# A pixel-transformer kernel on one core: among stages of several streams that are ready, the oldest stream's goes next instead of the one ready longest

## The reference

```python
# block 0
x = x + g_msa * attn(rope(q), rope(k), v, mask) @ attn_out_W      # self attention, 1024 x 1024
x = x + g_x * attn(qc, kc, vc) @ co_W                             # cross attention on 77 context rows
x = x + g_mlp * (gelu(xm @ mlp_W1 + b1) @ mlp_W2 + b2)
# block 1
x = x + sigmoid(gate) * (sum_e(router_e * silu(combined @ w1_e) @ w2_e) @ out_w + out_b)
# block 2, the same as block 0 with biases, full self attention over all 1024 keys, no rope
# block 3
x = x_q + attn(adaLN(x_q) @ Wq, k, v) @ Wp                        # cross attention again
```

## Time and profile before

| | us |
|---|---|
| median of 3 runs | 3506.51 (3498.44 to 3508.25) |
| the profiled execution, its own time | 3509.56 |
| its span, first to last instruction | 3507.8 |
| PE busy | 3309.1 |
| DVE busy | 1840.0 |
| ACT busy | 1434.7 |
| mean granted TensorE clock | 0.957 |

### The profile page before, as it was taken

How to read it: one execution, slowest core, us unless ns; L and a number is a source line. 1 busy time by engine, 2 the same in 40 slices (tenths; PEclk the granted TensorE clock), 3 DMA queues, 4 the chain that set the end, 5 groups by cost and what they waited for, 6 DMA issues and landing times.

```text
span 3507.8 us, 49090 instructions
## 1 busy us (share of the span) xinstructions
PE 3309.1 (94%) x19540; PEld 1824.3 (52%) x19540; DVE 1840.0 (52%) x3843; ACT 1434.7 (41%) x2607; POOL 244.4 (7%) x214
## 2 busy tenths in 40 slices
PE   6899999999889999998999999999999999999887
PEld 3555766657575666666333444544455344543364
DVE  4776554552412232324766765467755676556423
ACT  0344434353312222211355455554554645555433
POOL 1100100100100000001000010010100001010010
PEclk9999999989889999999899999999999999999897
DMA  5200000002000000001000000000000000000000
GB/s 166 90 6 1 9 20 4 25 1 95 16 22 1 0 1 0 1 1 55 1 1 1 1 7 4 1 25 7 7 4 16 10 7 7 4 16 16 1 1 13
DMA packets 57257, 57.99 MB, mean 17 GB/s; under 512 B 17728, under 2 KB 51249, under 8 KB 56765
## 3 DMA queue, kind: packets, MB, share of 16 engines
q1 hardware_dynamic: 57028, 54.79, 5.0%
HBM read 46.89 MB, written 7.89 MB: 16 GB/s over the span
## 4 chain that ended last, share of the span: by engine, by line
PE 90%; DVE 7%; ACT 2%; issue 1%; POOL 0%; DMA 0%; DVEq 0%; SPq 0%; ACTq 0%
PE ps L901 82%; PE ps L1075 3%; PE ps L1202 1%; PE ps L1055 1%; PE ps L1066 1%; DVE max_halves L1564 1%; DVE row_max_cross L1717 1%; ACT probs L1943 1%; DVE bn_stats L1618 1%; PE ps L1180 0%; ACT big L1895 0%; DVE big L1723 0%; DVE bn_stats L1595 0%; DVE xn_tok L1631 0%; DVE mean_var L1624 0%
## 5 line engine op out<-in xcount | busy, mean ns | idle before, releaser
L1895 ACT ACTIVATE big<-ps 128x512 f32<-128x512 f32 x1280 | 687.5, 597 | 809.4 <-PE ps L901 808.3
L901 PE MATMUL ps<-big 32*128 32x512 f32 (+2 forms) x5760 | 947.2, 605 | 14.7 <-DVE row_max L1561 4.3
L1564 DVE TENSOR_REDUCE max_halves<-ps 128x1 f32<-128x512 f32 x1024 | 652.8, 684 | 367.5 <-PE ps L901 366.7
L901 PEld LDWEIGHTS ps<-big 32*128 32x128 f32 (+1 forms) x5760 | 390.0, 189 | 496.2 <-issue 388.6
L901 PE MATMUL ps<-big,probs 128*32 128x512 f32 (+1 forms) x2688 | 379.0, 606 | 9.8 <-ACT big L1895 4.1
L901 PE MATMUL ps<-weights_mlp,big 128*128 128x256 f32 (+1 forms) x1248 | 336.0, 422 | 2.5 <-ACT big L1955 2.5
L901 PEld LDWEIGHTS ps<-weights_mlp,big 128*128 128x128 f32 x1248 | 236.9, 192 | 85.1 <-issue 57.1
L1601 DVE TENSOR_TENSOR x_tok<-ps,x_tok 128x512 f32<-128x512 f32 x112 | 77.3, 691 | 304.6 <-PE ps L901 304.6
L901 PE MATMUL ps<-x_T,weights_mlp 128*128 128x256 f32 x1024 | 229.8, 384 | 4.1 <-ACT x_T L1912 4.1
L1943 ACT ACTIVATE probs<-ps 77x512 f32<-77x512 f32 x384 | 196.1, 591 | 88.9 <-PE ps L901 88.9
L1561 DVE TENSOR_REDUCE row_max<-ps 128x2 f32<-128x512 f32 x256 | 165.0, 685 | 126.7 <-PE ps L901 126.3
(11 more groups left out here) (223 smaller groups left out, 3401.0 us busy)
## 6 DMA issues: line engine op xcount, KB each, us to landing
weights_mlp<-in_L_xcond_mlp_W SPq DMA_DIRECT2D x5, 1024.0 KB, 5.3
weights_mlp<-in_L_xcond_W_mlp SPq DMA_DIRECT2D x5, 1024.0 KB, 5.3
x_tok<-in_x SPq DMA_DIRECT2D x4, 1024.0 KB, 9.4
out_y<-x_tok SPq DMA_DIRECT2D x8, 512.0 KB, 2.9
big<-in_L_xcond_e_w SPq DMA_DIRECT2D x3, 1024.0 KB, 10.2
gates_biases<-mod_rows SPq DMA_DIRECT2D x20, 128.0 KB, 5.1
big<-in_L_xcond_adaLN_W SPq DMA_DIRECT2D x1, 2304.0 KB
kc_groups<-x_tok SPq DMA_DIRECT2D x3, 616.0 KB, 8.3
```

Source lines behind the costliest of these rows:

```text
L901: return pe.matmul(out, lhsT, rhs, start=first, stop=last)
L1564: dve.tensor_reduce(NMP[:, e, j, qt, hf:hf + 1], PS[:, bank, :], AX.X, ALU.max, negate=True).then_inc(R.frees(key), 1)
L1895: act.activation(PB[:, score % 2, j, :], PS[:, R.bank(key), :], ACT.Exp, scale=SCALE).then_inc(R.frees(key), 1)
```

## The change

Three lines of `overlapped` change, and one is added.

- The third key of the choice is the number of the stream instead of the time since which the stage has been ready. So of all `o_tokens` streams with a stage that can start, the oldest one's is placed.
- `cs` is now held back as well while a product of another half waits in `OTC` for its transposition. `state["holder"]` remembers whose product that is. A half may still place its own next `cs` between its `cp` and its `ct`.

```diff
-            state = {"now": 0.0, "t": -R.lead, "probs": 0, "turn": 0, "exp": 0.0, "credit": 0.0}
+            state = {"now": 0.0, "t": -R.lead, "probs": 0, "turn": 0, "exp": 0.0, "credit": 0.0, "holder": None}
...
                 if kind == "cs":
-                    return state["probs"] == 0
+                    return state["probs"] == 0 and (state["turn"] == 0 or state["holder"] == (tok[1], tok[2], tok[4]))
...
                     state["turn"] += {"cs": 0, "cp": 1, "ct": -1}[kind]
+                    state["holder"] = (tok[1], tok[2], tok[4]) if kind == "cp" else state["holder"]
...
-                work = sorted([f for f in found if f[0] <= now and cost(R, f[2])], key=lambda f: (not hidden_follows(f[2]), f[1] >= NB, f[0]))
+                work = sorted([f for f in found if f[0] <= now and cost(R, f[2])], key=lambda f: (not hidden_follows(f[2]), f[1] >= NB, f[1]))
```

## The result

The changed kernel takes 3495.86 us, the median of 18 runs (3484.44 to 3511.53). The kernel before takes 3509.19 us in 18 runs beside it (3498.44 to 3521.9). The ratio is **0.9971, 95% interval 0.996 to 0.9981**: about 10 us, or 0.29%, faster. (The two medians differ by 13 us, the means by 11. Runs of one kernel scatter by over 20 us, so the ratio with its interval is what counts.) The forecast was 3510.5 us, a gain of nothing. The time lies in the range that was given (3494 to 3526), but it was reached by a way that no part of the prediction described. Idle time went up as forecast, and the kernel got faster all the same.

The account below looks back on a forecast made before the run. PE was taken to bound the kernel, its work unchanged. Idle terms -2.6 + 2.0 - 2.4 + 1.0 + 4.1 = +2.1 us, x 1.93 = +4.1, on the median 3506.51 gave 3510.5 us; range 3494 to 3526.

Parts of the forecast that it names:

- Layer norm at the end of L0: L0's end piece: PE waits for normalized rows total 7.8 us in place of 3.45, +4.4 us.
- The other kinds there: L0's end piece: waits of `cs` -2.0, `cp` +1.7, `cm` -2.0, short ones -0.1 us; with layer norm +2.0.
- Middle of L2: `cm` directly behind a slot at 22 places in place of 11, usually waiting 0.76 us for exponentials: +4.1 us.
- Last slots of L0: Waits of 1.84 and 0.73 us both go, since `oP` and `oT` of older streams stand between the slots: -2.6 us.
- the rest of that middle: Middle of L0: twice a `cs` has only about 1.7 us between it and `cn`, +1.0 us for both.
- End of L2: L2's end piece: layer norm -2.7, `oT` -1.7, `cs` -1.3, `cp` +6.9, `cm` -2.7, short ones -0.9; together -2.4 us.
- The factor 1.93: Whole kernel: each us of idle time also brings 0.93 us of lost clock, so idle change is multiplied by 1.93.
- 32 products of `m1`: Example of the clock following idle time: they take 9.42 us right behind idle times, 7.14 us elsewhere.
- Tight places: Rival, slower: `ct` behind `cp` and one `cs` in the middles waits at every second place, 3529 us; chance 0.25.
- Table loads: Rival, slower: six more table loads on ACT, all ahead of something PE waits for, 3525 us; chance 0.05.
- Faster, end pieces shorter: Rival: waits on DVE in the end pieces vanish as bare counts say, 3487 us, half of it 3496; chance 0.20.

Follow-up runs that it names:

- the guard alone: The kernel before with only the new hold-back of `cs`, in both regions, and the old key of choice: 3510.68 us, ratio 1.0001.
- new middles alone: New key and hold-back of `cs` only until the last slot of a region, the old rule from there on, against the kernel before: 3512.45 us, ratio 1.0015.
- L0 alone: New key and hold-back of `cs` in L0, the old rule in L2, against the kernel before: 3503.45 us, ratio 0.9986.
- New ends alone: New key and hold-back of `cs` only behind the last slot of each region, against the kernel before: 3493.49 us, ratio 0.9947.
- L2's end alone: New key and hold-back of `cs` only behind the last slot of L2, against the kernel before: 3491.03 us, ratio 0.996.
- L0's end alone: New key and hold-back of `cs` only behind the last slot of L0, against the kernel before: 3512.64 us, ratio 1.0005.

## Why the prediction was wrong

**The idle time: right in its sign and in most of its terms.** The four pieces were to bring +2.1 us and brought +6.5, three times as much, though only 4.4 us more. The terms one by one:
- *Layer norm at the end of L0.* Forecast was one wait of 4.6 us, and `m1` behind it over 8 us. In the changed kernel, PE in order of time:

```profile
982.44 1.94 PE L1076 MATMUL ps<-ident,xn_tok 128*128 128x128 f32 x8 [4.49 <-DVE xn_tok L1632]
985.34 9.06 PE L902 MATMUL ps<-x_T,weights_mlp 128*128 128x256 f32 x32 [0.95 <-ACT x_T L1913]
```

  DVE and POOL just ahead of it. The normalization starts as soon as POOL is done:

```profile
980.82 1.03 POOL L2093 TENSOR_TENSOR rstd<-eps_tile,minus_half 128x4 f32<-128x4 f32 x1
981.88 1.38 DVE L1632 TENSOR_SCALAR xn_tok<-x_tok,mean_var,rstd 128x256 f32<-128x256 f32 x4 [1.47 <-POOL rstd L2093]
```

  All waits for `lnT` of that piece rose from 3.5 to 8.2 us, +4.7 (forecast +4.4). The other kinds there: `cs` -2.3 (-2.0), `cp` +1.8 (+1.7), `cm` -1.4 (-2.0).
- *Middle of L2.* +4.4 (forecast +4.1). The waits of `cm` are 33.2 us in place of 29.8, and those for a slot's exponentials in them 14.6 in place of 9.7:

```profile
L902 PE MATMUL ps<-k_v_cross,x_T 32*128 32x154 f32 x772 | 41.5, 329 | 33.2 <-ACT big L1896 14.6 <-DVE row_max_cross L1718 12.7 <-DVE max_halves L1565 5.8
```

- *Last slots of L0.* -2.6 was said. The 1.84 us is gone, but one of 0.72 us of the other kind stayed, so -1.85. In the rest of that middle `cm` won 3.8 us, and `oT` (+2.7), `cs` (+1.6, forecast +1.0) and `ct` (+1.3) took them back.
- *End of L2.* `cp` waits 11.1 us (forecast 11.7), and no layer norm waits any more (forecast 1.0 each for four). But `cm` waits 9.2 where I said 4.4, and the `cq` 4.4 where I put all short ones together at less than before. Of that, 2.6 us is one `cq` at 3387.3 us: DVE copies its rows only behind the statistics of another layer norm (1.40 and 0.38 us), a meeting that the sum had at nothing. So -2.4 became -0.4. The waits of `cp` near the end are as said:

```profile
3466.69 1.40 PE L902 MATMUL ps<-probs,k_v_cross 77*32 77x512 f32 x8 [1.72 <-ACT probs L1944]
...
3472.33 1.06 PE L902 MATMUL ps<-probs,k_v_cross 77*32 77x512 f32 x8 [1.38 <-ACT probs L1944]
```

**The factor 1.93: the step that failed.** I took 118 us of lost clock beside 126 us of idle time as 0.93 us per us, and so let the clock follow the *amount* of idle time. L2's end piece refutes it. In the two profiles, with idle time at 35.1 and 34.7 us, lost clock ((1 - clock) x length) is 35 us before and 10 after, 1.0 and 0.29 us per us. The size of that is partly luck, the finding isn't: over the four traces of each order without added products (the guard alone left out), mean idle time is 36.4 and 33.4 us and mean lost clock 30 and 20, where the factor ties 3 us of the one to 3 of the other. And the old order alone lost 35 us of clock at 35.1 us of idle time in one trace and 25 at 37.2 in another. The prediction had named a test, a clock that falls in a middle with idle time unchanged. In the middle of L0 it rose (0.96 to 0.97, idle 24.5 and 24.3), which breaks the tie just as well. By the factor, the measured +6.5 us of idle time would have cost 12.5 us more than before, 6 of them lost clock; in the timed runs lost clock fell by 17 us and the kernel got 10 us faster. What in an order sets its lost clock stays open. The windows above point to which stages stand beside the waits, and no run shows it. (The "32 products of `m1`" of the prediction are 32 records, 16 products. The sum doesn't use them.)

**The rivals.** *Tight places* (0.25) didn't come about: the waits of `ct` over the span are 3.7 us, not over 12.

```profile
L1203 PE MATMUL ps<-ident,o_T_cross 128*128 128x128 f32 x384 | 63.2, 288 | 3.7 <-ACT o_T_cross L1871 3.7
```

*Table loads* (0.05): there are six more ACT instructions on the page (2613 against 2607), each load still takes 1283 ns, and the wait that grew behind ACT, that of `cp`, is not theirs in the main: 7.6 of its 11.1 us in L2's end piece stand behind the last load of the kernel, which ends at 3429.7 us. Three of the six more are in the row below (25 before). The Trainium skill (ScalarE: Activation LUTs, What ACT_TABLE_LOAD costs) adds a drain of the engine to each switch; no run here isolates it.

```profile
L1956 ACT ACT_TABLE_LOAD x28 | 35.9, 1283 | 0.5
```

*Faster, end pieces shorter* (0.20) gave 3496 at half its size, and 3496 was measured. That is luck. Its mechanism, waits that vanish, is not what happened: together the two end pieces have 2.3 us more idle time.

**What stays open.**
- The middle of L0 is about 11 us shorter in the new order: 676.4 to 679.2 us in five traces against 688.2 to 691.4 in eight of the old one, at the same idle time. No run isolates what in the order does it. The kernel with new middles alone did not get faster by it (1.0015), and the end piece of L0 behind such a middle is longer, 184.0 to 187.6 us against 176.1 to 179.7. Taken whole, L0 is 862.4 us in the new order (two traces) and 866.6 in the old one (three), which fits L0 alone (0.9986).
- The parts do not add up exactly. New ends alone (0.9947) are faster than L2's end alone (0.996) and L0's end alone (1.0005) together, by about 6 us, and this is within their intervals.
- Whether the key or the guard makes L2's end piece shorter: the one trace with the guard alone has it as short. And whether long products between the short ones are what keeps the clock up: no run moves only those.
- Of the 19.7 us in L2's end piece, part is luck of this one profile. The three other traces of the new choice in this piece without added products have 207.9 to 209.2 us, those of the old one 212.2 to 218.5. By the means of the two (206.0 and 215.3) the change is worth some 9 us there. With the other pieces' -11 (L0 middle), +7 (L0 end) and +3 (L2 middle), taken in the same way, it comes to about -10, as the timed runs say. So it is the sum of pieces with both signs, and L2's end piece is only the largest. The four numbers are means of few traces each.

## What to carry to other kernels

Cost a new order twice: once in idle time, and once in lost clock. Do not tie the second to the first by one factor, since here the same idle time went with very different clocks; a stretch of short stages with waits between them can lose as much again as the waits themselves. In a tail of short stages with waits, a few unread products sized to the waits pay for themselves (0.9949 here on an order that was not changed at all), while those that overfill them don't (1.0021). Long products without a wait between the short ones may do the same (the clock was 1.00 in the windows that had them), but that was not tested alone. Before reading a gain of 0.3% out of two profiles, look at several executions: idle time of an order repeats, its clock does not. And try a rule of choice on the parts of a schedule separately: this one gains most behind the last slot of L2 and costs idle time in the middle of it.

## What the runs showed of the hardware

- The mean granted clock and the time of a run go together, within one kernel too. Over the repeated runs of a kernel the time falls by 1.9 to 3.5 us for each 0.001 of mean clock. The changed kernel's 18 runs have a mean clock of 0.963 where the kernel before has 0.958 in its runs beside the experiments.
- Idle time belongs to the order, the clock to the run. The middle of L0 in the old order has 24.3 to 24.6 us of idle time in eight traces, and 663.6 to 667.0 us of busy PE.
- Runs with one and the same instruction order in a piece differ almost by the clock alone. The middle of L2 in the new order took 1555.77 us in the changed kernel and 1542.87 in the one with new middles, at idle times of 44.2 and 45.1 us. A piece of one profile proves no change of 10 us. The Trainium skill (TensorE: Matmul & The Clock Gate, Part 1) says that the gate's state depends on how busy the array has lately been, and that the stretch at the lower clock differs from run to run of one kernel. The second agrees with these rows, and the first with the end pieces in which products filled waits (0.84 to 0.97 and 0.99).
- A float32 product of 128x128 is two records on PE. Nine in a row took 2.17 us, 0.24 us each; standing few together, 80 of them took 25.2 us, 0.32 each.
